# A third buffer of probability rows in fused graph attention, with the softmax two heads ahead and all of its normalising on GpSimd

## The chip, the core and the metric

The kernel runs on one NeuronCore of one Trainium2 chip. The core has five engines that run side by side, each through its own list of instructions in order: TensorE (PE in the profile; its weight loads are shown as PEld), VectorE (DVE), ScalarE (ACT), GpSimd (POOL) and SyncE (SP), which here only starts DMA transfers. An engine waits for another by a semaphore. The metric is the device time of one execution in microseconds (us), and lower is better.

## What is computed

A graph attention layer with 16 heads over 384 nodes, followed by a mixture of eight feed-forward experts. Only the attention is touched by the change. It is, cut from the reference:

```python
q2 = (q @ wiq.T + biq).reshape(N, H, D).transpose(1, 0, 2)   # N = 384, H = 16, D = 64; k2, v2 likewise
scores = jnp.einsum('hnd,hmd->hnm', q2, k2) * scale + mask[None]
attn = jax.nn.softmax(scores, axis=-1)
out = jnp.einsum('hnm,hmd->hnd', attn, v2)
out = out.transpose(1, 0, 2).reshape(N, OUT_F)
return out @ wo.T + bo
```

Everything is float32. The kernel keeps that precision by splitting each matmul operand into a high and a low part (`_hi`, `_lo`) and adding three products.

## The kernel before

The program has four parts that follow each other: six projections in twelve halves (to about 221 us), the attention heads (221.87 to 309.94 us), the output projection with the router (to about 380 us) and the experts. Each engine's order is written out by hand, in one function per engine; there is no scheduler. Semaphores are counted up, and a wait names the count that it needs.

The attention works head by head. A head has three row tiles of 128 nodes by 384 columns (`NT` = 3), and goes through these steps:

- `scores(h)` on TensorE (L1145): for each tile three products of 64 rows into PSUM banks B[0] to B[2]. Tile i of head h waits until `maxima` of head h-1 has read that bank (`score_max`).
- `maxima(h)` on VectorE (L818, L824): mask added, negated scores written to `pr`, row maximum taken. `pr` has two buffers, so head h waits until head h-2 has been transposed (`p_turned`).
- `exps(h)` on ScalarE (L587, L590): the exponential in place in `pr`, row sums into `rsum`.
- normalising: `inverse(h)` on VectorE (L837) takes the reciprocal of the first tile's sums, and GpSimd multiplies that tile (L446); `normalise(h)` on VectorE (L830, L832) takes the reciprocal of the other two and multiplies them itself.
- `turn(h)` on TensorE (L1154, L1161): nine transposes of 128x128 into banks B[3] to B[5], after all three tiles are normalised.
- `at_hi` on ScalarE (L607) and `at_lo` on VectorE (L858) copy the three turned tiles out as high and low part.
- `attend(h)` on TensorE (L1164): nine matmuls with v into bank B[6] or B[7]; then `t_hi` on ScalarE (L599) and `t_lo` on VectorE (L848).

TensorE's loop over h runs `turn(h)`, `attend(h-1)`, `scores(h+2)`. At h = 3, ScalarE and VectorE also split one 1 MB weight chunk for the output projection (L545 and L712, 128x2048); the other chunks of that kind are split after the heads. When `attend(15)` is done (`o_ready` = 16), GpSimd starts `memset(brow_f)` (L451), some constants, and then three additions to `xres` (L471), which VectorE needs for the residual (L881). SyncE's loads of the residual wait for the last scores (L351), those of the output bias for the last `attend` (L356).

Of the kernel before, what the change touches and what calls it, by code (L numbers as in the profile page):

```python
# [30 lines left out]
F32 = mybir.dt.float32  # L31
# [75 lines left out]
def gnn_ffn(nc, x, src, dst, ety, srcb, dstb, ew, wg, bcols, bo, lng, lnb, rw, egc, ebc, wf, b1, b2, be, out):  # L107
    ctx = ExitStack()
    with ctx:
# [19 lines left out]
        with gnn:  # L129
# [7 lines left out]
            with ExitStack() as early:  # L137
                xin = sb(early, "xin", [P, NT, D], F32)
                src_i = sb(early, "src_i", [P, 2, PIECE * P], I32)
                dst_i = sb(early, "dst_i", [P, 2, PIECE * P], I32)  # L140
                keyb = sb(early, "keyb", [P, PIECE * P], F32)
                eqt = sb(early, "eqt", [P, 2, WIN * P], F32)
            k_hi = sb(gnn, "k_hi", [P, KT, N], F32R)
            k_lo = sb(gnn, "k_lo", [P, KT, N], F32R)
            pr = sb(gnn, "pr", [P, 2, NT, N], F32)
# [4 lines left out]
            wterm = sb(gnn, "wterm", [P, 4, EG], F32)  # L150
            bits = sb(gnn, "bits", [P, 2, EG], I32)
            dump = sb(gnn, "dump", [P, EG], F32)
            later = sb(gnn, "later", [P, WIN * P], F32)
# [82 lines left out]
        first_inverse, first_normalised = sem("first_inverse"), sem("first_normalised")  # L236
# [39 lines left out]
        negmax = small[:, 52:58].rearrange("p (b i) -> p b i", b=2)  # L276
        rsum = small[:, 58:64].rearrange("p (b i) -> p b i", b=2)

        rinv = small[:, 64:70].rearrange("p (b i) -> p b i", b=2)
# [125 lines left out]
        def _(pool):  # L405
# [123 lines left out]
        def _(act):  # L529
# [57 lines left out]
            def exps(h):  # L587
                for i in range(NT):
                    act.wait_ge(score_max, NT * h + i + 1)
                    act.activation(pr[:, h % 2, i, :], pr[:, h % 2, i, :], ACT.Exp, scale=-1.0,  # L590
                                   bias=negmax[:, h % 2, i:i + 1], accum_out=rsum[:, h % 2, i:i + 1]).then_inc(exp_done, 1)

            exps(0)
            for h in range(HEADS + 2):
                if h >= 2:

                    o, rows = h - 2, slice(HD * (h % 2), HD * (h % 2) + HD)
                    act.wait_ge(o_ready, o + 1)
                    act.activation(t_hi[rows, o // 2, :], B[6 + h % 2][rows, 0:N], ACT.Identity,  # L599
                                   bias=gbias[rows, 1, o // 2:o // 2 + 1]).then_inc(o_hi_done, 1)  # L600
# [7 lines left out]
                if h + 1 < HEADS:  # L608
                    exps(h + 1)
# [92 lines left out]
        def _(dve):  # L702
# [115 lines left out]
            def maxima(h):  # L818

                if h >= 2:  # L820
                    dve.wait_ge(p_turned, NT * (h - 1))
                for i in range(NT):
                    dve.wait_ge(score_ready, NT * h + i + 1)
                    dve.tensor_tensor_reduce(out=pr[:, h % 2, i, :], in0=B[i][:, 0:N], in1=mask8[:, i, :],  # L824
                                             scale=-SCALE8, scalar=BIG, op0=ALU.add, op1=ALU.min,
                                             accum_out=negmax[:, h % 2, i:i + 1]).then_inc(score_max, 1)

            def normalise(h):
                dve.wait_ge(exp_done, NT * (h + 1))
                link(dve.reciprocal(rinv[:, h % 2, 1:NT], rsum[:, h % 2, 1:NT]))  # L830
                for i in range(1, NT):
                    dve.tensor_scalar(pr[:, h % 2, i, :], pr[:, h % 2, i, :], rinv[:, h % 2, i:i + 1], None,  # L832
                                      ALU.mult).then_inc(normalised, 1)

            def inverse(h):
                dve.wait_ge(exp_done, NT * h + 1)
                dve.reciprocal(rinv[:, h % 2, 0:1], rsum[:, h % 2, 0:1]).then_inc(first_inverse, 1)  # L837
# [566 lines left out]
```

## Time and profile before

| | |
|---|---|
| median of 3 runs | 569.07 us (567.72 to 569.13) |
| the profiled execution | 569.24 us, span 567.5 us |
| busy in the span | PE 513.8 us (91%), DVE 407.6 (72%), ACT 282.3 (50%), POOL 149.1 (26%) |
| mean granted TensorE clock | 0.949 of full |
| chain that ended last | PE 60%, DVE 19%, ACT 8%, POOL 4%, no instruction ("issue") 6% |

The profile covers one execution. Times in a timeline are from the start of the span; the duration of a matmul in it is modelled and overlaps the next, so a run of matmuls is timed from start to start. The chain of waits follows back from the last instruction what released it. The table of stretches gives each engine's busy time within a stretch, and as PEclk the granted clock of TensorE as a part of full speed: 1.00 is 2.4 GHz and 0.50 is 1.2 GHz, its two levels, and what lies between is a stretch with some of both.

### The profile page before, as it was taken

How to read it: one execution, taken by the hardware profiler on the slowest of the kernel's cores; microseconds unless marked ns; L12 is line 12 of the kernel's file. 1: busy time of each engine (PE TensorE's matmuls, PEld its weight loads, DVE VectorE, ACT ScalarE, POOL GpSimd, SP SyncE). 2: the span in 40 equal slices, each digit the busy share in tenths (PEclk: the TensorE clock that was granted, in tenths of full speed). 3: DMA queues.
4: the chain of work that ended last, by engine and by line, in shares of the span. 5: the costliest groups of instructions: out<-in, count | busy, mean ns of one | idle time of the engine just before them, and what ended most of it. 6: DMA issues, size and time to landing. Idle time of an engine off the chain costs nothing.

```text
span 567.5 us, 6818 instructions
## 1 busy us (share of the span) xinstructions
PE 513.8 (91%) x2579; PEld 445.8 (79%) x2579; DVE 407.6 (72%) x675; ACT 282.3 (50%) x407; POOL 149.1 (26%) x129
## 2 busy tenths in 40 slices
PE   3899999999999998989998979449999999999994
PEld 3899889999999998878787868437776776776773
DVE  6658877744334435789997867775987987987995
ACT  2435223423323443677776104335787687687540
POOL 5100333542334330122223922222012022000362
PEclk9899999999999999689999989658999999999988
DMA  8278663333443343010006521495859889879452
GB/s 308 107 267 361 230 234 136 118 130 126 150 149 105 118 151 114 1 74 2 0 1 209 179 62 69 137 343 205 319 220 397 318 328 390 330 288 374 149 185 112
DMA packets 20929, 106.32 MB, mean 187 GB/s; under 512 B 4720, under 2 KB 5104, under 8 KB 11168
## 3 DMA queue, kind: packets, MB, share of 16 engines
q1 hardware_dynamic: 15328, 91.53, 42.6%
q0 software_dynamic: 3696, 7.96, 4.3%
q10 hardware_dynamic: 1872, 6.39, 3.1%
q8 instruction: 21, 0.34, 0.2%
q14 instruction: 12, 0.10, 0.1%
HBM read 98.96 MB, written 6.91 MB: 187 GB/s over the span
## 4 chain that ended last, share of the span: by engine, by line
PE 60%; DVE 19%; ACT 8%; issue 6%; POOL 4%; DMA 1%; ACTq 0%; DVEq 0%; POOLq 0%
PE ps L1098 53%; DVE lo L712 10%; PE ps L1161 3%; ACT xg L629 3%; POOL xres L471 2%; ACT hi L545 2%; PE ps L1201 2%; DVE hh L1022 1%; ACT xg_hi L633 1%; DMA xg<-z_rows,slot_tok 1%; DVE small L717 1%; ACT sg L638 1%; DMA xin<-in_x 1%; DVE x2c L1011 1%; DVE ht_lo L977 1%
## 5 line engine op out<-in xcount | busy, mean ns | idle before, releaser
L712 DVE TENSOR_TENSOR lo<-raw,hi 128x2048 fp32r<-128x2048 f32 x70 | 159.2, 2289 | 60.6 <-ACT hi L545 60.5
L545 ACT ACTIVATE hi<-raw 128x2048 fp32r<-128x2048 f32 x70 | 131.7, 1913 | 76.0 <-PE ps L1098 65.1
L438 POOL DMA_INDIRECT mask_rows<-colf,bits x48 | 56.2, 1171 | 134.7 <-DMA mask_rows<-colf,bits 83.0
L1098 PE MATMUL ps<-xt_hi,hi 128*128 128x384 f32 x192 | 65.2, 339 | 2.3 <-DVE xt_lo L728 2.3
L1098 PE MATMUL ps<-xt_hi,lo 128*128 128x384 f32 x192 | 65.2, 340 | 0.0
L1098 PE MATMUL ps<-xt_lo,hi 128*128 128x384 f32 x192 | 65.2, 340 | 0.0
L1098 PE MATMUL ps<-hi,xg_hi 128*128 128x512 f32 x128 | 53.1, 415 | 1.5 <-DVE xg_lo L972 1.5
L1098 PE MATMUL ps<-lo,xg_hi 128*128 128x512 f32 x128 | 51.3, 401 | 0.0
L1098 PE MATMUL ps<-hi,xg_lo 128*128 128x512 f32 x128 | 51.2, 400 | 0.0
L1098 PE MATMUL ps<-t_hi,lo 128*128 128x384 f32 x128 | 43.0, 336 | 0.0
L1098 PE MATMUL ps<-t_lo,hi 128*128 128x384 f32 x128 | 43.0, 336 | 0.0
L1098 PE MATMUL ps<-t_hi,hi 128*128 128x384 f32 x128 | 43.0, 336 | 0.0
L446 POOL TENSOR_SCALAR pr<-pr,small 128x384 f32<-128x384 f32 x16 | 19.9, 1246 | 76.2 <-DVE small L837 76.2
L1098 PE MATMUL ps<-hi,t_hi 128*128 128x512 f32 x96 | 39.0, 406 | 0.0
L1098 PEld LDWEIGHTS ps<-xt_hi,hi 128*128 128x128 f32 x192 | 36.7, 191 | 2.6 <-issue 2.6
L1098 PE MATMUL ps<-hi,t_lo 128*128 128x512 f32 x96 | 38.6, 402 | 0.0
L1098 PE MATMUL ps<-lo,t_hi 128*128 128x512 f32 x96 | 38.6, 402 | 0.0
L1098 PEld LDWEIGHTS ps<-xt_hi,lo 128*128 128x128 f32 x192 | 36.6, 191 | 0.0
L1098 PEld LDWEIGHTS ps<-xt_lo,hi 128*128 128x128 f32 x192 | 36.5, 190 | 0.0
L1098 PEld LDWEIGHTS ps<-hi,xg_hi 128*128 128x128 f32 x128 | 24.7, 193 | 10.8 <-issue 5.6
L607 ACT ACTIVATE at_hi<-ps 128x384 fp32r<-128x384 f32 x48 | 20.7, 492 | 24.0 <-PE ps L1161 23.1
L1161 PE MATMUL ps<-ident,pr 128*128 128x128 f32 x144 | 21.8, 303 | 9.9 <-issue 3.9
(207 smaller groups left out, 1065.8 us busy)
## 6 DMA issues: line engine op xcount, KB each, us to landing
raw<-in_wf SPq DMA_DIRECT2D x42, 1024.0 KB, 7.2
raw<-in_wg SPq DMA_DIRECT2D x28, 1024.0 KB, 5.4
xfb<-in_wf SPq DMA_DIRECT2D x6, 1024.0 KB, 7.3
src_i<-in_srcb ACTq DMA_DIRECT2D x4, 768.0 KB, 4.9
dst_i<-in_dstb ACTq DMA_DIRECT2D x4, 768.0 KB, 9.9
y_rows<-y SPq DMA_DIRECT2D x6, 512.0 KB, 3.0
xin<-in_x SPq DMA_DIRECT2D x3, 512.0 KB, 4.6
xres<-in_x SPq DMA_DIRECT2D x3, 512.0 KB, 4.8
```

The costliest lines, as they stand in the source:

```text
L438: pool.indirect_dma_start(out=mbuf[:, :], out_offset=bass.IndirectOffsetOnAxis(ap=bits[:, 1, g:g + 1], axis=0), in_=colf[:, 5, g:g + 1], i ...
L446: pool.tensor_scalar(pr[:, h % 2, 0, :], pr[:, h % 2, 0, :], rinv[:, h % 2, 0:1], None, ALU.mult).then_inc(first_normalised, 1)
L471: pool.tensor_tensor(xres[:, t, :], xres[:, t, :], bob, ALU.add).then_inc(resid_ready, 1)
L545: act.activation(hi[SLOT[c]][:, :], raws[RAW[c]], ACT.Copy).then_inc(hi_done, 1)
L607: act.activation(at_hi[:, h % 2, j, :], B[3 + j][:, 0:N], ACT.Copy).then_inc(at_hi_done, 1)
L629: ins = act.activation(xg[:, par, k * P:(k + 1) * P], B[5 + a][:, (k % 4) * P:(k % 4 + 1) * P], ACT.Identity, scale=egb[:, 0, e, k:k + 1], ...
L633: act.activation(xg_hi[:, par, 4 * a:4 * a + 4, :].rearrange("p k n -> p (k n)"), xg[:, par, a * CW:(a + 1) * CW], ACT.Copy).then_inc(xg_h ...
L638: act.activation(sg[:, :], x2c[:, :], ACT.Silu).then_inc(silu_done, 1)
L712: dve.tensor_tensor(lo[SLOT[c]][:, :], raws[RAW[c]], f32(hi[SLOT[c]][:, :]), ALU.subtract).then_inc(lo_done, 1)
L1098: ins = pe.matmul(o, a[s], b[m], start=first and n == 0, stop=last and n == 2)
L1161: ins = pe.transpose(B[3 + j][:, i * P:(i + 1) * P], pr[:, h % 2, i, j * P:(j + 1) * P], ident[:, :])
L1201: ins = pe.matmul(B[0][:, t * NE:(t + 1) * NE], xft[:, k, :], rws[:, k, :], start=k == 0, stop=k == KT - 1)
```

## The change

`pr` and the small columns beside it (`negmax`, `rsum`, `rinv`) get a third buffer, indexed by h % 3. To make room, three tensors that are used only before the attention (`wterm`, `dump`, `later`) move to memory that k_hi and its neighbours reuse. TensorE issues `scores(h+3)` instead of `scores(h+2)`, with `scores(2)` ahead of the loop. ScalarE does `exps(h+2)` instead of `exps(h+1)`, and `t_hi` of a head at the end of a turn of its loop instead of at the start of the next. VectorE does `maxima(h+2)` and only the reciprocals, in two instructions; the multiplications L832 are gone from it. GpSimd does three multiplications for each head instead of one. The diff, without the moved tensors:

```diff
-            pr = sb(gnn, "pr", [P, 2, NT, N], F32)
+            pr = sb(gnn, "pr", [P, 3, NT, N], F32)
...
             for h in range(HEADS):
-                pool.wait_ge(first_inverse, h + 1)
-                pool.tensor_scalar(pr[:, h % 2, 0, :], pr[:, h % 2, 0, :], rinv[:, h % 2, 0:1], None,
-                                   ALU.mult).then_inc(first_normalised, 1)
+                for i in range(NT):
+                    if i < 2:
+                        pool.wait_ge(inverse_ready, 2 * h + i + 1)
+                    pool.tensor_scalar(pr[:, h % 3, i, :], pr[:, h % 3, i, :], rinv[:, h % 3, i:i + 1], None,
+                                       ALU.mult).then_inc(normalised, 1)
...
             exps(0)
-            for h in range(HEADS + 2):
-                if h >= 2:
-
-                    o, rows = h - 2, slice(HD * (h % 2), HD * (h % 2) + HD)
-                    act.wait_ge(o_ready, o + 1)
-                    act.activation(t_hi[rows, o // 2, :], B[6 + h % 2][rows, 0:N], ACT.Identity,
-                                   bias=gbias[rows, 1, o // 2:o // 2 + 1]).then_inc(o_hi_done, 1)
+            exps(1)
+            for h in range(HEADS + 1):
                 if h == 3:
                     split_hi(OUT_LAST - 1)
...
-                if h + 1 < HEADS:
-                    exps(h + 1)
+                if h + 2 < HEADS:
+                    exps(h + 2)
+                if h >= 1:
+
+                    o, rows = h - 1, slice(HD * ((h - 1) % 2), HD * ((h - 1) % 2) + HD)
+                    act.wait_ge(o_ready, o + 1)
...
-                if h >= 2:
-                    dve.wait_ge(p_turned, NT * (h - 1))
+                if h >= 3:
+                    dve.wait_ge(p_turned, NT * (h - 2))
...
+            def inverse(h, tiles, done):
+                dve.wait_ge(exp_done, NT * h + done)
+                dve.reciprocal(rinv[:, h % 3, tiles], rsum[:, h % 3, tiles]).then_inc(inverse_ready, 1)
+
+            FIRST_TILE, OTHERS = (slice(0, 1), 1), (slice(1, NT), NT)
             maxima(0)
-            inverse(0)
-            normalise(0)
+            inverse(0, *FIRST_TILE)
+            maxima(1)
+            inverse(0, *OTHERS)
+            inverse(1, *FIRST_TILE)
+            inverse(1, *OTHERS)
             for h in range(HEADS + 2):
-                if h + 1 < HEADS:
-                    maxima(h + 1)
+                if h + 2 < HEADS:
+                    maxima(h + 2)
...
                     for j in range(NT):
-                        if j == NT - 1 and h + 1 < HEADS:
-                            inverse(h + 1)
+                        if j == NT - 1 and h + 2 < HEADS:
+                            inverse(h + 2, *FIRST_TILE)
...
-                if h + 1 < HEADS:
-                    normalise(h + 1)
+                if h + 2 < HEADS:
+                    inverse(h + 2, *OTHERS)
...
             def turn(h):
-                pe.wait_ge(first_normalised, h + 1)
-                pe.wait_ge(normalised, (NT - 1) * (h + 1))
+                pe.wait_ge(normalised, NT * (h + 1))
...
             scores(0)
             scores(1)
+            scores(2)
             for h in range(HEADS + 1):
                 if h < HEADS:
                     turn(h)
                 if h >= 1:
                     attend(h - 1)
-                if h + 2 < HEADS:
-                    scores(h + 2)
+                if h + 3 < HEADS:
+                    scores(h + 3)
```

VectorE within one head in the middle, before. The names are the tiles: `t_lo` is the output of an earlier head, `at_lo` the low part of the turned tiles of head h, `small` the columns of sums and reciprocals; the L824 rows at the end begin `maxima` of the next head.

```order
L848 SCALAR_TENSOR_TENSOR t_lo<-ps,gbias,t_hi 64x384 [waits o_hi_done]
L858 TENSOR_TENSOR at_lo<-ps,at_hi 128x384 [waits at_hi_done] x2
L837 RECIPROCAL small<-small 128x1 [waits exp_done]
L858 TENSOR_TENSOR at_lo<-ps,at_hi 128x384 [waits at_hi_done]
L830 RECIPROCAL small<-small 128x2 [waits exp_done]
L832 TENSOR_SCALAR pr<-pr,small 128x384 [waits dve_chain]
L832 TENSOR_SCALAR pr<-pr,small 128x384
L824 ISA pr,small<-ps,mask 128x384 [waits score_ready,p_turned]
```

The same place in the changed kernel (L827 is the old L824, L833 both reciprocals):

```order
L848 SCALAR_TENSOR_TENSOR t_lo<-ps,gbias,t_hi 64x384 [waits o_hi_done]
L858 TENSOR_TENSOR at_lo<-ps,at_hi 128x384 [waits at_hi_done] x2
L833 RECIPROCAL small<-small 128x1 [waits exp_done]
L858 TENSOR_TENSOR at_lo<-ps,at_hi 128x384 [waits at_hi_done]
L833 RECIPROCAL small<-small 128x2 [waits exp_done]
L827 ISA pr,small<-ps,mask 128x384 [waits score_ready,p_turned]
```

The two multiplications L832 are gone, and the reciprocals now belong to head h+2 instead of h+1.

TensorE at the start of the attention, before: the last tile of `scores(1)`, `turn(0)`, and the first tile of `scores(2)`. `k_hi` and `xt_hi` are keys and queries, `ident,pr` is a transpose.

```order
L1098 MATMUL ps<-k_hi,xt_hi 128x384 [waits score_max]
L1098 MATMUL ps<-k_lo,xt_hi 128x384
L1098 MATMUL ps<-k_hi,xt_lo 128x384
L1161 MATMUL ps<-ident,pr 128x128 [waits normalised,first_normalised]
L1161 MATMUL ps<-ident,pr 128x128 x8
```

The same piece in the changed kernel, where the rows ahead of `turn(0)` are the last two tiles of `scores(2)`:

```order
L1098 MATMUL ps<-k_hi,xt_hi 128x384 [waits score_max]
L1098 MATMUL ps<-k_lo,xt_hi 128x384
L1098 MATMUL ps<-k_hi,xt_lo 128x384
L1098 MATMUL ps<-k_hi,xt_hi 128x384 [waits score_max]
L1098 MATMUL ps<-k_lo,xt_hi 128x384
L1098 MATMUL ps<-k_hi,xt_lo 128x384
L1160 MATMUL ps<-ident,pr 128x128 [waits normalised]
```

The nine matmuls of `scores(2)` stand ahead of `turn(0)` instead of behind it, and every `scores` after that is one head earlier. GpSimd's list has 48 multiplications (L448) in place of 16 (L446), and the rest of it is unchanged, as is SyncE's.

## Rows read from the trace of the kernel before

**Rows 1.** Table of stretches, cut at starts of `turn`: stretch, length, busy time (count), PEclk, DMA

```profile
221.87:238.53 16.66, 15.23 (x63) 13.58 (x63) 11.52 (x39) 9.44 (x26) 3.77 (x3) 0.69 0.00 0
238.53:243.24 4.71, 4.57 (x29) 4.03 (x28) 3.79 (x13) 4.07 (x11) 1.24 (x1) 1.00 0.01 3
243.24:250.32 7.08, 4.53 (x28) 3.98 (x28) 6.95 (x16) 4.94 (x11) 1.25 (x1) 0.98 0.21 74
250.32:256.30 5.98, 5.98 (x28) 5.47 (x28) 4.83 (x17) 3.84 (x10) 1.24 (x1) 0.73 0.22 89
256.30:295.70 39.40, 36.26 (x217) 31.90 (x217) 36.39 (x111) 28.94 (x80) 9.95 (x8) 1.00 0.00 1
295.70:300.78 5.08, 4.52 (x27) 3.98 (x28) 4.77 (x15) 3.63 (x10) 1.25 (x1) 1.00 0.00 0
300.78:305.61 4.83, 2.77 (x19) 2.48 (x19) 4.45 (x15) 3.61 (x10) 1.24 (x1) 1.00 0.91 314
305.61:309.94 4.33, 4.33 (x28) 4.33 (x29) 2.65 (x5) 1.83 (x4) 0.00 (x0) 1.00 0.76 254
```

**Rows 2.** Chain of waits, one head: start, length, what

```profile
265.98 1.18 PE ps L1161 x9
267.15 3.35 PE ps L1098 x18
270.50 0.56 issue
```

**Rows 3.** Timeline, two heads: start, length, engine, line, operation [idle before]

```profile
260.31 0.75 DVE L832 TENSOR_SCALAR pr<-pr,small 128x384 f32<-128x384 f32 x2
...
264.10 1.24 POOL L446 TENSOR_SCALAR pr<-pr,small 128x384 f32<-128x384 f32 x1 [3.69 <-DVE small L837]
...
264.98 0.90 DVE L832 TENSOR_SCALAR pr<-pr,small 128x384 f32<-128x384 f32 x2
```

**Rows 4.** Groups by line, 224 to 308 us: busy us, mean ns | idle before

```profile
L590 ACT ACTIVATE pr<-pr,small 128x384 f32<-128x384 f32 x48 | 29.0, 612 | 1.2 <-DVE small L824 1.1
...
L824 DVE CUSTOM_DVE_ANT_0 pr<-ps,mask 128x384 f32<-128x384 f32 x46 | 23.1, 548 | 0.2 <-PE ps L1098 0.2
...
L607 ACT ACTIVATE at_hi<-ps 128x384 fp32r<-128x384 f32 x48 | 20.7, 492 | 24.0 <-PE ps L1161 23.1
```

**Rows 5.** GpSimd's multiplication, line L446 alone: ns min/median/max, first and last start

```profile
L446 POOL TENSOR_SCALAR pr<-pr,small x16: 1242/1244/1263, 224.5 to 303.7; 128x384 f32<-128x384 f32 x16
```

**Rows 6.** GpSimd's longest instructions after the heads, line L471 alone: ns min/median/max

```profile
L471 POOL TENSOR_TENSOR xres<-xres,xfb x3: 3392/3874/4452, 315.5 to 322.7; 128x1024 f32<-128x1024 f32 x3
```

**Rows 7.** Timeline at the start of the attention

```profile
224.26 0.16 DVE L837 RECIPROCAL small<-small 128x1 f32<-128x1 f32 x1
...
224.54 1.26 POOL L446 TENSOR_SCALAR pr<-pr,small 128x384 f32<-128x384 f32 x1 [15.66 <-DVE small L837]
...
225.36 0.17 DVE L830 RECIPROCAL small<-small 128x2 f32<-128x2 f32 x1 [0.94 <-ACT pr L590]
...
226.48 2.15 PE L1161 MATMUL ps<-ident,pr 128*128 128x128 f32 x9 [1.20 <-DVE pr L832]
```

**Rows 8.** Table of stretches where the granted clock was low

```profile
226.60:236.20 9.60, 9.37 (x34) 8.56 (x35) 6.98 (x23) 6.22 (x17) 1.86 (x2) 0.50 0.00 0
...
247.70:250.20 2.50, 0.06 (x1) 0.00 (x0) 2.46 (x8) 0.51 (x2) 1.25 (x1) 0.98 0.57 197
250.20:253.20 3.00, 2.88 (x12) 2.91 (x13) 2.89 (x10) 1.68 (x4) 0.00 (x0) 0.50 0.46 186
```

**Rows 9.** Timeline of the weight chunk that is split at h = 3

```profile
242.78 1.92 ACT L545 ACTIVATE hi<-raw 128x2048 fp32r<-128x2048 f32 x1
...
245.25 2.29 DVE L712 TENSOR_TENSOR lo<-raw,hi 128x2048 fp32r<-128x2048 f32 x1
```

**Rows 10.** Chain of waits after the last head

```profile
309.99 1.80 POOL brow_f L451
...
315.50 11.62 POOL xres L471 x3
```

More of the change, by code:

```diff
@@ L142, in gnn_ffn @@
                 eqt = sb(early, "eqt", [P, 2, WIN * P], F32)
+                wterm = sb(early, "wterm", [P, 4, EG], F32)
+                dump = sb(early, "dump", [P, EG], F32)
+                later = sb(early, "later", [P, WIN * P], F32)
             k_hi = sb(gnn, "k_hi", [P, KT, N], F32R)
             k_lo = sb(gnn, "k_lo", [P, KT, N], F32R)
-            pr = sb(gnn, "pr", [P, 2, NT, N], F32)
+            pr = sb(gnn, "pr", [P, 3, NT, N], F32)
             at_hi = sb(gnn, "at_hi", [P, 2, NT, N], F32R)
@@ L275, in gnn_ffn @@
         halfneg = small[:, 48:49]
-        negmax = small[:, 52:58].rearrange("p (b i) -> p b i", b=2)
-        rsum = small[:, 58:64].rearrange("p (b i) -> p b i", b=2)
-        rinv = small[:, 64:70].rearrange("p (b i) -> p b i", b=2)
+        negmax = small[:, 52:61].rearrange("p (b i) -> p b i", b=3)
+        rsum = small[:, 61:70].rearrange("p (b i) -> p b i", b=3)
+        rinv = small[:, 0:9].rearrange("p (b i) -> p b i", b=3)
         SCALE8 = 1.0 / 8.0
@@ L818, in maxima @@
             def maxima(h):
[L820 to L821 removed]
+                if h >= 3:
+                    dve.wait_ge(p_turned, NT * (h - 2))
                 for i in range(NT):
                     dve.wait_ge(score_ready, NT * h + i + 1)
[L824 removed]
+                    dve.tensor_tensor_reduce(out=pr[:, h % 3, i, :], in0=B[i][:, 0:N], in1=mask8[:, i, :],
                                              scale=-SCALE8, scalar=BIG, op0=ALU.add, op1=ALU.min,
[L826 to L837, printed above, removed]
[L839 to L841 removed]
+                                             accum_out=negmax[:, h % 3, i:i + 1]).then_inc(score_max, 1)
+            def inverse(h, tiles, done):
+                dve.wait_ge(exp_done, NT * h + done)
+                dve.reciprocal(rinv[:, h % 3, tiles], rsum[:, h % 3, tiles]).then_inc(inverse_ready, 1)
+            FIRST_TILE, OTHERS = (slice(0, 1), 1), (slice(1, NT), NT)
+            maxima(0)
+            inverse(0, *FIRST_TILE)
[3 more added lines that the diff above has]
+            inverse(1, *OTHERS)
             for h in range(HEADS + 2):
[L843 to L844 removed]
+                if h + 2 < HEADS:
+                    maxima(h + 2)
                 if h >= 2:
@@ L1160, in turn @@
                     for i in range(NT):
-                        ins = pe.transpose(B[3 + j][:, i * P:(i + 1) * P], pr[:, h % 2, i, j * P:(j + 1) * P], ident[:, :])
+                        ins = pe.transpose(B[3 + j][:, i * P:(i + 1) * P], pr[:, h % 3, i, j * P:(j + 1) * P], ident[:, :])
                     ins.then_inc(p_turned, 1)
```

11 lines of the change are left out of this document (5 added, 6 removed).

## The prediction, made before the changed kernel was run

> **What bounds the kernel now.** I read the table of stretches first, cut at the starts of `turn`, because only the attention changes. The last matmul of the attention starts it off at 221.87 us and ends it at 309.94 us, 88.07 us in all [rows 1]. In the middle, the eight heads from `turn(5)` to `turn(13)` take 39.40 us, 4.925 us each. VectorE is busy for 36.39 us of that and TensorE for 36.26 us [rows 1], so two engines look full. The chain of waits tells them apart: nine transposes take 1.18 us and the eighteen matmuls behind them 3.35 us, 4.53 us in all, and then TensorE stands for up to 0.56 us [rows 2]. That is a loop over three engines. After `turn(h)` ScalarE copies the tiles (3 x 0.49 us) and then takes the exponentials of head h+1 (3 x 0.61 us) [rows 4], VectorE then multiplies two tiles (0.75 us, or 0.90 us in the next head) [rows 3], and only then can `turn(h+1)` go. TensorE's own 4.53 us is the floor underneath.
>
> Three more places lose time. The first two heads up to `turn(2)` take 16.66 us, at a mean clock of 0.69 [rows 1]: the granted clock was 0.50, that is 1.2 GHz, for 9.60 us [rows 8], after TensorE had stood for 1.20 us ahead of `turn(0)` [rows 7]. Head 3 takes 7.08 us [rows 1], since the weight chunk holds ScalarE for 1.92 us and then VectorE for 2.29 us [rows 9] in the same loop; TensorE stands idle for nearly all of 2.50 us, and the clock is then 0.50 for 3.00 us more [rows 8], so head 4 takes 5.98 us. At the end, the heads after `turn(13)` take 5.08 and 4.83 us up to `turn(15)`, though the second has only 2.77 us of TensorE work [rows 1].
>
> What is behind the attention hangs on its end: GpSimd starts at 309.99 us and runs into the 11.62 us of `xres` additions [rows 10]. SyncE's list is the same, its residual loads wait for the last scores, which come a head earlier, and all else for the last `attend`. A gain in the attention passes on in full.
>
> **The middle.** Removed from VectorE are two multiplications per head, 0.75 to 0.90 us [rows 3]; 36.39 / 8 = 4.55 us of work becomes 3.65 to 3.80. ScalarE does the same work, 28.94 / 8 = 3.62 us per head [rows 1]. GpSimd goes from one to three multiplications, 3 x 1.244 = 3.73 us [rows 5]; a handover from the reciprocal took 224.54 - 224.42 = 0.12 us [rows 7], so at most 3.97. All are under 4.53.
>
> Does the loop still hold? Count from the start of `turn(h)`. The copies are done at about 1.8 us (0.55 us until the first, then 3 x 0.42 from start to start, an estimate from the length of three overlapping instructions), the exponentials of head h+2 at 1.8 + 1.9 = 3.7, the reciprocals at 3.9, and GpSimd's last two tiles at 3.9 + 0.1 + 2 x 1.244 = 6.5, call it 6.6. They are needed at `turn(h+2)`, at 9.06. `maxima(h+2)` can start when the reciprocals of head h+1 are done, 3.9 - 4.53 = -0.6, and ends near 0.6 behind the last score tile; ScalarE asks for it at 1.8, and `scores(h+3)` at 2.8. What queues behind the new waits of VectorE, the third `at_lo` and the next `maxima`, has 1 us to spare or more. So nothing is late, and TensorE's 4.53 us becomes the period: from `turn(5)` to `turn(13)` 39.40 - 36.24 = **3.2 us gained**. For the period I keep 4.40 to 4.60 as bounds: 4.40 if some of the 3.35 us still holds small waits, 4.60 if 0.07 is lost between `scores` and `turn`, where the trace shows no boundary without a wait.
>
> **Heads 2 to 4.** `turn(2)` to `turn(3)` took 4.71 us, 0.2 over the period. At h = 3 ScalarE now has 0.2 us in hand, so its copies come 1.7 us late and end at 3.0 us after `turn(3)`. VectorE does the chunk from 1.75 to 4.05 us, then two `at_lo` to 5.1 and the third to 5.65. `turn(4)` may begin at 4.53 and needs those banks freed one by one: it ends about 0.4 us late. The exponentials of head 5 are not wanted for another head. With this wait shortened to 0.4 us the idle 2.5 us and the low clock behind it go as well. Here one unknown remains: this subtraction reads two SBUF tensors while GpSimd is busy far more than before. The nearest row is GpSimd's L471, which took 3392 to 4452 ns [rows 6] with VectorE busy beside part of it, so neighbours may cost something. GpSimd's tiles for head 4 end about 2.05 us after `turn(3)` and its next begin at 5, so the two would meet for 0.3 us. I take 0.3, with 0 and one whole multiplication, 1.25 us, as bounds. Total stall 0.7 us. `turn(2)` to `turn(5)` goes from 17.77 [rows 1] to 3 x 4.53 + 0.7 = 14.3: **3.5 us gained**.
>
> On this place the Trainium skill (SBUF — State Buffer, "Who interferes with whom") says that a VectorE instruction with two SBUF inputs contends with a GpSimd instruction that reads SBUF, and that the later one stands until the other is through. By that rule the stall would be 0.4 plus whatever is left of one multiplication; and the pair L832, which took 0.90 us when it began at 264.98 beside a GpSimd multiplication that ran until 265.34, and 0.75 us in the head before, agrees in kind [rows 3]. [...]
>
> **The tail.** `turn(15)` now waits for GpSimd, not for TensorE: `maxima(15)` and `exps(15)` lie in turn 13 of the loops, so by the count above it starts 6.6 us after `turn(13)`, where TensorE alone would need 2 x (1.18 + 1.76) = 5.9. It took 5.08 + 4.83 = 9.91 us [rows 1]. **3.3 us gained.** The last 4.33 us stay.
>
> **The start** goes the other way. `scores(2)` and `maxima(1)` move ahead of the second reciprocal of head 0, which could be made at 225.36 [rows 7] and now follows three L824 at some 0.48 us from start to start, at 226.1. GpSimd's first tile ends at 225.8 [rows 7], the others at 226.2 + 2 x 1.25 = 228.7, so `turn(0)` starts at 228.75 instead of 226.48 [rows 7]. Head 1's three tiles end at 228.7 + 3.75 = 232.45, head 2's at 236.2. TensorE stands from 226.5 to 228.75, and in both places of the trace where it stood the clock came back at half [rows 7, 8]. At half, `turn(0)` takes 2.15 [rows 7], `scores(3)` 3.0, and `turn(1)` runs from 233.9. If the clock returns at 236.4 as in the trace (the low 9.60 us [rows 8] plus its edges), `turn(2)` starts at 239.4; with a first transpose block still at full speed 239.1. If it returns after about 3 us, as in the second place [rows 8], 237.5; with no drop at all 237.0, by GpSimd's pace; with ten low us that start later, 240.5. I take 239.0, near the longer case since that is the same place of the program: **0.5 us lost**, although one more `scores` is done by then (which the tail gives back).
>
> **Sum.** 3.2 (middle) + 3.5 (heads 2 to 4) + 3.3 (tail) - 0.5 (start) = 9.5 us. The attention ends at 300.4, and the profiled 569.24 us become **559.7 us**. The profiled execution is 0.17 us above the median of the three runs, 569.07, so no correction is made. Its own range: start 237.0 to 240.5, stall 0.4 to 1.65, period 4.40 to 4.60 over eleven heads, and 1 us of spread behind the attention as the runs have (567.72 to 569.13); not all at one end, 557.0 to 563.
>
> **Rivals.** (a) The low clock comes back. TensorE was busy for 9.37 of 9.60 us and stayed at 0.50 [rows 8], so work alone did not raise it at once; the many heads at 1.00 [rows 1] speak against. A second such stretch costs half of 10.2 us: 559.7 + 5.1 = 564.8. (b) Another loop holds the heads near 4.9 us, for instance VectorE's waits in the middle of its list: 11 x 0.4 = 4.4 us of the gain is gone, 564.1. The slack of 1 us counted above speaks against. (c) GpSimd is slowed by its neighbour as L471 may have been, 1.244 x 4452 / 3392 = 1.63 us per tile: 48 x 1.63 from 224.54 is 302.8, with handovers 304.5, near the old `turn(15)` at 305.6. That is 568. All sixteen multiplications ran in 1242 to 1263 ns [rows 5] beside VectorE's work, which speaks against. (d) Slower: each GpSimd multiplication first has to wait out a VectorE instruction, 0.55 us [rows 4]: 1.79 us a tile, 48 x 1.79 + 224.54 = 310.5 against 305.61, 4.9 us later, 574.1. This mechanism decides the sign from (305.61 - 224.54) / 48 = 1.69 us a tile; the measured 1.244 is far below.
>
> **How the numbers follow.** Forecast 72%, (a) 9%, (b) 9%, (c) 5%, (d) 5%. Faster by over 0.3% (1.7 us, about what a measurement of this kernel can tell from no change) are the forecast, (a) and (b): 0.90. Same is (c): 0.05. Slower is (d): 0.05. The range must leave out no more than 20%. It leaves out (c), (d), the longer half of (a), and the edge of the forecast: 557.0 to 564.5.
>
> **What would show it.** In the changed kernel: `turn` every 4.5 to 4.6 us from `turn(5)` on with no idle time of TensorE ahead of it; L448 at 1.24 to 1.3 us, three in a row; no gap of 2.5 us at h = 3 and a clock of 1.00 around 250 us; `turn(0)` near 228.7 with idle time released by POOL; GpSimd as what ends the wait of `turn(15)`; the last `attend` near 300.4. A period over 4.7 or an L448 over 1.45 us would prove the middle wrong, a clock of 0.50 after 240 us the start.

## The result, and the profile after

| | before | after |
|---|---|---|
| median, us | 569.09 | 559.28 |
| lowest to highest, runs | 567.72 to 569.13, 4 | 558.90 to 561.25, 4 |
| profiled execution, us | 569.24 | 561.25 |
| its span, us | 567.5 | 559.5 |
| attention, first scores to last matmul | 88.07 | 79.51 |

The ratio of the times is 0.983 [0.981, 0.985], so the changed kernel is 9.8 us faster; 559.7 was predicted. The profiled execution is the longest of the four. Two other profiles of the same kernel (first experiment) have an attention that is 1.6 us shorter, all of it in the first two heads. Their first scores come 1.3 to 1.5 us later (at 222.96 and 222.77 us, not 221.51), so their spans are only 0.8 and 0.9 us shorter. The part of the span behind the attention is 257.5 us before and 258.4 in this profile (257.7 and 257.9 in the other two): the gain does pass on, to within 0.9 us.

Here is the table of stretches of the changed kernel, cut at the starts of `turn`, with the columns of [rows 1]. After the stretch and its length come the busy time (and count) of PE, PEld, DVE, ACT and POOL, and then PEclk, DMA and GB/s. The cuts are at the first scores, `turn(0)`, `turn(1)`, `turn(2)`, `turn(3)`, `turn(4)`, `turn(5)`, `turn(13)` and `turn(15)`:

```profile
221.51:228.22 6.71, 4.92 (x28) 4.52 (x28) 4.72 (x21) 4.14 (x13) 3.80 (x4) 1.00 0.00 0
228.22:233.45 5.23, 5.23 (x19) 4.46 (x19) 2.66 (x10) 3.26 (x9) 5.23 (x5) 0.51 0.00 0
233.45:240.34 6.89, 6.89 (x29) 6.19 (x29) 3.68 (x12) 3.84 (x10) 5.34 (x5) 0.63 0.01 2
240.34:244.90 4.56, 4.56 (x29) 4.06 (x29) 3.65 (x13) 3.99 (x11) 2.27 (x3) 1.00 0.00 0
244.90:249.50 4.60, 4.39 (x27) 3.85 (x27) 4.29 (x8) 4.58 (x11) 1.78 (x2) 1.00 0.01 2
249.50:254.28 4.78, 4.78 (x28) 3.97 (x29) 4.78 (x19) 4.21 (x11) 4.29 (x4) 1.00 0.61 219
254.28:290.12 35.84, 35.84 (x218) 31.81 (x218) 30.66 (x99) 28.96 (x80) 30.68 (x26) 1.00 0.01 1
290.12:296.65 6.53, 5.33 (x36) 4.87 (x36) 5.46 (x15) 5.33 (x14) 5.53 (x5) 1.00 0.81 283
296.65:301.02 4.37, 4.37 (x28) 4.37 (x29) 2.42 (x5) 1.83 (x4) 0.00 (x0) 1.00 0.47 177
```

A cut may stand 0.14 us beside the true start: the timeline has `turn(2)` at 240.28, `turn(3)` at 244.76, `turn(5)` at 254.21 and `turn(13)` at 290.05. I use those below. In the seventh row TensorE is busy for all of 35.84 us, where [rows 1] had 36.26 of 39.40; VectorE has fallen from 36.39 to 30.66 us and GpSimd has risen from 9.95 to 30.68 us. No wait of another engine is left. The chain of waits (start, length, what) in the middle and at the end says the same, and answers to [rows 2, 10]:

```profile
258.76 1.13 PE ps L1160 x9
259.90 3.36 PE ps L1098 x18
263.25 1.13 PE ps L1160 x9
...
292.91 3.70 POOL pr L448 x3
296.61 0.04 issue
296.65 1.20 PE ps L1160 x9
297.86 3.16 PE ps L1098 x18
301.02 0.05 issue
301.07 1.80 POOL brow_f L453
```

Nine transposes and eighteen matmuls now stand edge to edge, 1.13 + 3.36 = 4.49 us a head. In this piece only `turn(15)` hangs on GpSimd's three multiplications, which take 3.70 us with nothing between them. The line of that multiplication alone (ns min/median/max, first and last start) answers to [rows 5]:

```profile
L448 POOL TENSOR_SCALAR pr<-pr,small x48: 1239/1246/1264, 224.2 to 295.4; 128x384 f32<-128x384 f32 x48
```

Forty-eight of them, and the longest took 1264 ns: none was held up by VectorE. The timeline of the start and of the weight chunk (start, length, engine, line, operation, idle time before it and what ended it) answers to [rows 7, 9]:

```profile
228.22 2.11 PE L1160 MATMUL ps<-ident,pr 128*128 128x128 f32 x9 [1.79 <-POOL pr L448]
...
243.00 3.69 POOL L448 TENSOR_SCALAR pr<-pr,small 128x384 f32<-128x384 f32 x3 [2.29 <-DVE small L833]
...
246.47 2.29 DVE L715 TENSOR_TENSOR lo<-raw,hi 128x2048 fp32r<-128x2048 f32 x1 [0.25 <-ACT hi L547]
...
249.50 1.45 PE L1160 MATMUL ps<-ident,pr 128*128 128x128 f32 x9 [0.21 <-DVE at_lo L858]
```

The first line is the new wait at `turn(0)`: 1.79 us for GpSimd, and the nine transposes behind it take 2.11 us instead of the 1.20 that this view gives them at full clock, since the clock is at half. The last line is all that is left of the 2.50 us that TensorE stood at h = 3 [rows 8]: 0.21 us for the third `at_lo`.

### The profile page after: what moved, and what is told of

Same layout as the page of the kernel before. It is cut to its first block, busy times and chain, and to the rows that moved or that the text cites. A ratio compares the mean times of both kernels' runs of the same rounds, so it can differ in the third digit from the quotient of the medians.

```text
span 559.5 us, 6816 instructions
## 1 busy us (share of the span) xinstructions
PE 513.0 (92%) x2579; PEld 445.1 (80%) x2579; DVE 394.6 (71%) x643; ACT 282.3 (50%) x407; POOL 187.7 (34%) x161
## 4 chain that ended last, share of the span: by engine, by line
PE 60%; DVE 19%; ACT 9%; issue 6%; POOL 5%; DMA 1%; ACTq 0%; DVEq 0%; POOLq 0%
PE ps L1098 53%; DVE lo L715 10%; ACT xg L632 3%; PE ps L1160 3%; ACT hi L547 2%; POOL xres L473 2%; PE ps L1201 2%; POOL pr L448 1%; DVE hh L1022 1%; ACT xg_hi L636 1%; DMA xg<-z_rows,slot_tok 1%; PE ps L1194 1%; DVE small L720 1%; ACT sg L641 1%; DVE x2c L1011 1%
## 5 line engine op out<-in xcount | busy, mean ns | idle before, releaser
L448 POOL TENSOR_SCALAR pr<-pr,small 128x384 f32<-128x384 f32 x48 | 58.9, 1247 | 29.3 <-DVE small L833 29.3
L492 POOL CAST selx<-sels 48x128 fp32r<-48x128 f32 x8 | 3.4, 436 | 93.7 <-PE ps L1098 89.7
L592 ACT ACTIVATE pr<-pr,small 128x384 f32<-128x384 f32 x48 | 29.0, 612 | 1.2 <-DVE small L827 1.1
```

Of the source, the lines that this page charges most:

```text
L448: pool.tensor_scalar(pr[:, h % 3, i, :], pr[:, h % 3, i, :], rinv[:, h % 3, i:i + 1], None, ALU.mult).then_inc(normalised, 1)
L592: act.activation(pr[:, h % 3, i, :], pr[:, h % 3, i, :], ACT.Exp, scale=-1.0, bias=negmax[:, h % 3, i:i + 1], accum_out=rsum[:, h % 3, i:i ...
```

## Experiments

The question of all of them: the change has two halves, a deeper pipeline and a move of two multiplications from VectorE to GpSimd. Which one brings the gain, and what does each cost? The theory on record is that the loop over three engines set the old period, so depth would do it. The first rival is that VectorE, at 36.39 of 39.40 us [rows 1], was the bound, and the move does it. "Attention" is from here on from the first scores to the start of `brow_f` on GpSimd, 88.12 us before.

### The changed kernel again

No edit. Two more groups of runs, on other occasions (the second beside the last two versions below), to see which part of the first profile repeats.

> The changed kernel once more, unaltered, as the pair for the runs beside it and for a second profile. Expected 558.9 to 561.3 us. The first profile is of the longest of four executions: from the end of the last attend (301.02 us) to the end of the span it took 258.5 us, against 257.6 us in the kernel before. If that 0.9 us is chance, as I think, this profile has 257 to 258 us there and the attention still ends near 301; if it belongs to the change, it has 258.5 again.

Measured: 560.19 us (559.05 to 560.68), ratio 0.982 [0.980, 0.984]. The attention took 78.00 us, where the first profile had 79.56. The first three stretches:

```profile
222.96:229.68 6.72, 4.91 (x28) 4.53 (x28) 4.73 (x21) 4.13 (x13) 3.80 (x4) 1.00 0.00 0
229.68:233.63 3.95, 3.95 (x19) 3.35 (x19) 2.10 (x8) 3.03 (x9) 3.95 (x4) 0.70 0.00 0
233.63:240.18 6.55, 6.55 (x28) 6.06 (x28) 4.08 (x14) 3.83 (x10) 6.27 (x6) 0.66 0.01 3
```

`turn(0)` comes 6.72 us after the first scores, as before; what differs is how the low clock falls on what follows (0.70 and 0.66, against 0.51 and 0.63). In the first profile the granted clock was 0.50 from 228.4 to 238.5 us, 10.1 us from the first transposes on. Here the transposes of `turn(0)` run at full speed, and it is 0.50 from about 231.3 to 238.0 us, 6.7 us. `turn(2)` is 17.22 us after the start, not 18.77. Behind the attention this profile has 257.7 us, so most of the 0.9 us more of the first one does not repeat and is no cost of the change. The other group repeats all this.

> The changed kernel once more, on the same chip as the runs beside it: 559 to 560.5 us.

Measured: 559.45 us (559.10 to 560.35), ratio 0.983 [0.981, 0.985]; attention 77.98 us, `turn(2)` 17.20 us after the start. So 78.0 us is the usual attention of this kernel, and the first profile's 1.6 us more is a variation of when the clock is low. I don't know what decides that.

### Depth alone

Three buffers and the new order stay. GpSimd multiplies only the first tile, as before the change, and VectorE the other two; `turn` waits for both.

```diff
-                for i in range(NT):
+                for i in range(1 if h in VECTOR else NT):      # VECTOR = range(HEADS)
...
+            def others(h):
+                inverse(h, *OTHERS)
+                if h in VECTOR:
+                    dve.wait_ge(inverse_ready, 2 * h + 2)
+                    for i in range(1, NT):
+                        dve.tensor_scalar(pr[:, h % 3, i, :], pr[:, h % 3, i, :], rinv[:, h % 3, i:i + 1], None,
+                                          ALU.mult).then_inc(vector_normalised, 1)
...
-                    inverse(h + 2, *OTHERS)
+                    others(h + 2)
...
```

> One part alone: three buffers, scores three ahead and softmax two ahead stay, but VectorE multiplies the second and third tile of every head again (from its own list, after their reciprocals) and GpSimd only the first. My theory: the gain comes from the depth, which takes the loop ScalarE, VectorE, TensorE apart; the move to GpSimd is only there to get VectorE's work per head (3.8 us in the changed kernel, 4.55 us with the two multiplications) under TensorE's 4.48. So the period is 4.5 to 4.75 us and the time 555 to 563 us, with a turn(0) near 226.5 us instead of 228.2 as an extra. Rival: the gain comes from the unloading of VectorE; then the period stays at 4.9 us and the time at 563 us or more.

Measured: 559.35 us (559.20 to 560.27), ratio 0.982 [0.980, 0.984]; attention 78.09 us. The stretches are the first two heads, then head 3 and head 4, then the eight of the middle, then the two of the tail:

```profile
221.81:235.08 13.27, 12.34 (x73) 10.93 (x73) 11.87 (x43) 10.84 (x32) 4.03 (x4) 1.00 0.00 0
...
239.57:245.91 6.34, 4.53 (x28) 3.98 (x28) 6.21 (x14) 5.17 (x11) 0.99 (x1) 1.00 0.00 1
245.91:252.18 6.27, 6.27 (x27) 5.28 (x28) 6.20 (x20) 3.87 (x10) 2.49 (x2) 0.73 0.46 167
252.18:288.01 35.83, 35.83 (x217) 31.80 (x216) 35.33 (x110) 29.11 (x80) 8.81 (x8) 1.00 0.01 1
288.01:295.32 7.31, 5.80 (x37) 4.91 (x37) 7.17 (x21) 5.02 (x13) 2.46 (x2) 1.00 0.85 284
```

The middle is 35.83 us with the move undone: the same 4.48 us a head for TensorE. So it was the loop that held the heads at 4.93 us, and not the length of VectorE's list. But VectorE is now the next bound, and it is already the slower of the two. Its pair of multiplications in the turn of the loop ahead of `turn(5)` and the one eight heads later, and then TensorE at `turn(14)` (start, length, engine, line, operation, idle time before it and what ended it):

```profile
251.37 0.99 DVE L841 TENSOR_SCALAR pr<-pr,small 128x384 f32<-128x384 f32 x2
...
288.45 0.99 DVE L841 TENSOR_SCALAR pr<-pr,small 128x384 f32<-128x384 f32 x2
...
292.26 1.44 PE L1172 MATMUL ps<-ident,pr 128*128 128x128 f32 x9 [1.48 <-DVE at_lo L867]
```

VectorE needs 37.08 / 8 = 4.64 us a head, so it falls 0.16 us a head behind TensorE and lives on the lead that the depth gives it. The debt comes due in the tail, where `turn(14)` stands for 1.48 us until the third `at_lo`. With many more heads VectorE would set the pace, by these rows at 4.64 us (an estimate); with the move it is busy for 30.66 / 8 = 3.83 us a head. All versions with three buffers also have `t_hi` at its new place in ScalarE's loop and the scores three heads ahead; what each of these is worth alone was not tested, and "depth" here means all of them together.

The total is equal to that of the changed kernel because differences cancel. At the start depth alone is better by 3.9 us (`turn(2)` 13.27 us after the first scores, not 17.2, at a clock of 1.00). At the weight chunk it is worse by about 3.2 us (heads 3 and 4 take 12.61 us, 9.45 with the move), since VectorE has no slack from which to pay the 2.29 us of the subtraction, and in the tail by 0.7 (7.31 against 6.60).

### The move alone

Two buffers, one head ahead, the old order, and GpSimd multiplies all three tiles.

```diff
-                pool.wait_ge(first_inverse, h + 1)
-                pool.tensor_scalar(pr[:, h % 2, 0, :], pr[:, h % 2, 0, :], rinv[:, h % 2, 0:1], None,
-                                   ALU.mult).then_inc(first_normalised, 1)
+                for i in range(NT):
+                    if i < 2:
+                        pool.wait_ge(inverse_ready, 2 * h + i + 1)
+                    pool.tensor_scalar(pr[:, h % 2, i, :], pr[:, h % 2, i, :], rinv[:, h % 2, i:i + 1], None,
+                                       ALU.mult).then_inc(normalised, 1)
...
-                for i in range(1, NT):
-                    dve.tensor_scalar(pr[:, h % 2, i, :], pr[:, h % 2, i, :], rinv[:, h % 2, i:i + 1], None,
-                                      ALU.mult).then_inc(normalised, 1)
```

> The other part alone: the kernel before with two buffers and the softmax one head ahead, but GpSimd multiplies all three tiles. My theory: two multiplications of 1.25 us then stand in the loop in place of 0.8 us on VectorE, so turn comes every 6.5 to 6.7 us and the time is 590 to 600 us, more if TensorE's clock falls in the waits. Rival (unloading VectorE is what helped): 569 us or less.

Measured: 597.94 us for its one run, some 29 us slower than before; attention 115.27 us, some 6.5 us a head. Its chain of waits walks once round the loop in a head:

```profile
263.97 0.56 PE ps L1159 x3
...
264.56 1.26 ACT at_hi L609 x3
...
265.83 0.72 ACT pr L592 x2
...
266.58 0.17 DVE small L836
...
266.83 3.70 POOL pr L448 x3
```

This is the loop of the prediction's first part, with GpSimd's three multiplications in place of VectorE's two. In the changed kernel the same 3.70 us sit in the same place and cost nothing in the middle, because one more head of TensorE's work lies between the exponentials and the `turn` that needs them. Moving work to a slower engine without the depth loses three times what the change gains.

### How near GpSimd is to being the bound

Rival (c) said that GpSimd's pace could decide. Two more multiplications per head, which alter nothing that is read later, bring it over the 4.49 us of TensorE.

```diff
+                for cut in (slice(0, 6), slice(0, 2)):
+                    link(pool.tensor_scalar(colf[:, cut, :], colf[:, cut, :], rinv[:, h % 3, 0:1], None, ALU.mult))
```

> The changed kernel, with two more multiplications by GpSimd behind the three of each head, on 288 and 96 columns of a tensor that is no longer needed (colf), each awaited. GpSimd's work per head goes from 3.75 us to about 5.2 us (estimate: 0.95 and 0.4 us for the two, 0.1 for each wait). My theory: GpSimd has 0.7 us to spare below TensorE's 4.48 us, and from there on sets the period alone; turn(15) starts at 224.2 + 15 x 5.25 + 3.7 = 306.7 us instead of 296.6, and the time is near that of the kernel before, 567 to 571 us. Rival (another engine still holds the period, GpSimd's work is hidden up to 5 us): under 563 us.

Measured: 576.01 us (575.85 to 576.17), ratio 1.011 [1.009, 1.013]: slower than before the change, and past what I expected. One head in the chain of waits, then the line alone, then the timeline at the weight chunk:

```profile
264.22 3.69 POOL pr L448 x3
267.90 0.98 POOL colf L451
...
268.98 0.53 POOL colf L451
```

```profile
L448 POOL TENSOR_SCALAR pr<-pr,small x48: 1237/1244/3042, 224.5 to 309.6; 128x384 f32<-128x384 f32 x48
```

```profile
246.30 5.48 POOL L448 TENSOR_SCALAR pr<-pr,small 128x384 f32<-128x384 f32 x3
...
247.16 2.29 DVE L717 TENSOR_TENSOR lo<-raw,hi 128x2048 fp32r<-128x2048 f32 x1 [0.25 <-ACT hi L549]
```

GpSimd's head is 3.69 + 0.98 + 0.53 us and 0.17 us between them, 5.37 us, and `turn` follows at 5.37 us from its start to the next. The mechanism is right, and the size was not: I had given a head 5.25 us. `turn(15)` came at 310.94 us and not at 306.7, mostly by 0.12 us a head and the one long multiplication below, and TensorE then took 6.07 us to the end at a clock of 0.72, where the changed kernel took 4.37. By these rows, per head GpSimd has 4.49 - 3.70 = 0.8 us in hand, and beyond that it sets the pace; only the one point beyond was tested.

One multiplication took 3042 ns. The three ran from 246.30 to 251.78, so by the lengths the second began near 247.55, with VectorE's subtraction of two SBUF tensors under way until 249.45. Standing until then and taking 1.2 us would end it at 250.65; 247.55 + 3.04 is 250.59. That is the rule of the Trainium skill (SBUF — State Buffer, "Who interferes with whom") that the prediction weighed, in numbers: 1.8 us lost by the later one. The other direction doesn't show. In the changed kernel that subtraction began at 246.47 with GpSimd busy until 243.00 + 3.69 = 246.69, and here at 247.16 with GpSimd's first multiplication running until about 247.54, and it took 2.29 us both times, the mean of its line. It may be that the overlap was too short to see.

### VectorE for head 0 alone

The start is where GpSimd's three tiles in a row are on the path. So the edit of "Depth alone", with one head:

```diff
-        VECTOR = range(HEADS)
+        VECTOR = (0,)
```

> The changed kernel, with the second and third tile of head 0 alone multiplied by VectorE. Theory: TensorE's 1.8 us of standing ahead of turn(0), while GpSimd works through three tiles, is what brings the granted clock down to 1.2 GHz for some 10 us; with turn(0) at 226.7 us, as in e_depth, the clock stays at 1.00, turn(1) waits for GpSimd until 230.6, turn(2) starts near 235.1 instead of 240.3, and the time is 553.5 to 555 us. Rival: e_depth kept its clock since VectorE paced all heads; then the clock falls here too, turn(2) starts at 239 or later, and the time is over 558 us.

Measured: 555.98 us (555.12 to 557.37), ratio to before 0.977 [0.975, 0.979], so 3 to 4 us under the changed kernel. The expected 553.5 to 555 was missed upward, though the heads did what the theory said: the part behind the attention took 258.5 us in this profile. Up to `turn(0)`, `turn(1)` and `turn(2)`:

```profile
222.93:227.88 4.95, 4.90 (x28) 4.47 (x28) 3.97 (x17) 3.84 (x12) 1.27 (x1) 1.00 0.00 0
227.88:231.75 3.87, 2.96 (x19) 2.47 (x19) 3.28 (x14) 3.33 (x11) 3.76 (x4) 1.00 0.00 0
231.75:236.24 4.49, 4.49 (x27) 3.98 (x27) 3.81 (x14) 3.50 (x10) 4.49 (x4) 1.00 0.00 0
```

`turn(0)` starts 4.95 us after the first scores with no wait to speak of, the clock stays at 1.00, and `turn(2)` comes at 13.31 us, not 17.2. The attention is 74.11 us.

### Transposes that fill the wait

That gain has two causes mixed: the wait itself, and the low clock after it. This separates them. GpSimd keeps all tiles, and sixteen identity transposes into a free bank keep TensorE at work until `turn(0)`.

```diff
+            keep_warm(B[6], 16)        # after scores(2), ahead of turn(0)
```

> The changed kernel, with 16 transposes of the identity into an unused bank (B[6]) between scores(2) and turn(0), which is 1.7 us of work at full speed in the 1.8 us in which TensorE stood. Theory: the clock then stays at 1.00; turn(0) does not start earlier, turn(1) is released by GpSimd at about 232.0 and turn(2) starts near 236.5 instead of 240.3: 555 to 556.5 us. Rival (the low clock comes from what TensorE does before turn(0), not from the standing): low clock as before, 559 to 561 us.

Measured: 556.70 us (555.39 to 557.96), ratio 0.978 [0.976, 0.979]; attention 75.65 us.

```profile
221.73:228.44 6.71, 6.71 (x43) 6.21 (x43) 4.73 (x21) 4.13 (x13) 3.79 (x4) 1.00 0.00 0
228.44:232.10 3.66, 2.98 (x19) 2.49 (x18) 1.79 (x7) 3.03 (x9) 3.66 (x4) 1.00 0.00 0
```

`turn(0)` stands where it stood, 6.71 us after the start, and the clock stays at 1.00. So the low clock costs 78.00 - 75.65 = 2.35 us of the changed kernel, and the wait for GpSimd in head 0 a further 75.65 - 74.11 = 1.54 us. These are differences between single profiles. The whole times agree on the first (the expected 555 to 556.5 was missed by 0.2 us); the second, 556.70 against 555.98, is too small for them.

The same in the kernel before, with eleven transposes:

> The kernel before, with 11 such transposes between scores(1) and turn(0), in place of 1.2 us of standing. It tells how much of the 9.8 us the clock alone is worth without the change. Theory: the clock stays at 1.00 there, and the first two heads are then paced by the loop at 4.9 us each: turn(2) at 236.4 instead of 238.5, 2 us less than the kernel before, 566.5 to 568 us. Rival: the low clock is the main loss of the kernel before, 564 us or less.

Measured: 569.49 us (566.43 to 570.32), ratio 1.000 [0.998, 1.001]. A miss. The first row below runs from `turn(0)` to `turn(2)`, which comes 13.96 us after the first scores at 222.59, not 16.66 [rows 1], with the clock at 1.00: 2.7 us earlier. Then it gives it all back:

```profile
227.20:236.55 9.35, 7.46 (x47) 6.46 (x46) 7.75 (x27) 6.53 (x19) 2.51 (x2) 1.00 0.00 0
...
248.45:255.61 7.16, 7.16 (x27) 6.47 (x28) 5.15 (x17) 3.84 (x10) 1.25 (x1) 0.59 0.20 82
...
304.95:310.93 5.98, 5.98 (x28) 5.95 (x29) 2.75 (x5) 2.02 (x5) 0.00 (x0) 0.71 0.54 184
```

Head 4 takes 7.16 us at 0.59, where it was 5.98 at 0.73 [rows 1], and the last stretch 5.98 at 0.71, where it was 4.33 at 1.00. The idle 2.5 us of head 3 and the wait ahead of `turn(15)` are still there, and the low clock now stands behind both. In this kernel the repair of this one wait did not pay; in the changed kernel, where only the 1.2 us ahead of `turn(15)` are left besides, it does.

### VectorE for the first and the last head

The tail, too, waits for three GpSimd tiles in a row.

```diff
-        VECTOR = (0,)
+        VECTOR = (0, HEADS - 1)
```

> As e_start, and also the second and third tile of head 15 by VectorE. Theory: turn(15) then waits for nothing and starts 5.9 us after turn(13) instead of 6.5; 0.6 us less than e_start, 553 to 554.5 us. Rival: turn(15) was held by something besides GpSimd, and it stays at 6.5.

Measured: 556.03 us (555.04 to 557.59), ratio 0.977 [0.975, 0.979]. From `turn(13)` to `turn(15)` it is

```profile
284.83:290.71 5.88, 5.42 (x37) 4.99 (x37) 5.11 (x15) 5.18 (x14) 3.17 (x3) 1.00 0.75 265
```

5.88 us against 6.60. That is not yet TensorE alone, as the expectation had it: `turn(15)` now stands for the third `at_lo`:

```profile
290.71 1.39 PE L1172 MATMUL ps<-ident,pr 128*128 128x128 f32 x9 [0.47 <-DVE at_lo L867]
```

The attention is 73.56 us, 0.55 less than with head 0 alone, but the median is not lower, and the expected 553 to 554.5 us was missed: half a microsecond can't be told in the whole time. A second group of runs of the same version:

> e_ends once more, unaltered, on the same chip: 3 to 4 us less than the changed kernel beside it. Its attention took 73.56 us, against 79.56 and 78.00 us in two profiles of the changed kernel.

Measured: 556.12 us (554.74 to 557.68), ratio 0.976 [0.974, 0.979], with the changed kernel at 559.45 beside it: 3.3 us below it.

### One tile of each head for VectorE

GpSimd takes the first and the third tile of every head, VectorE the second. Against the changed kernel, with `others` as above:

```diff
-                for i in range(NT):
-                    if i < 2:
-                        pool.wait_ge(inverse_ready, 2 * h + i + 1)
+                for i in (0, 2):
+                    pool.wait_ge(inverse_ready, 2 * h + 1 + i // 2)
...
-                    for i in range(1, NT):
+                    for i in (1,):
```

> The changed kernel, with the work of normalising split evenly in every head: GpSimd multiplies the first and third tile, VectorE the second. Theory: VectorE's work per head is then 3.8 + 0.4 = 4.2 us and GpSimd's 2.5 us, both under TensorE's 4.48; turn(0) comes 5.3 us after the first scores (6.7 in the changed kernel, 4.95 in e_ends), so TensorE stands for 0.5 us only and the clock stays at 1.00; turn(15) comes 5.9 us after turn(13). The attention takes 74 us against 78.0 to 79.6 in the changed kernel, and the time is 554.5 to 556.5 us. Rival: VectorE's multiplication meets GpSimd's at the memory port (0.99 us for two in e_depth beside GpSimd, 0.75 alone) in each head, and the period rises to 4.6 us or more: 557 us or more.

Measured: 555.62 us (554.37 to 557.31), ratio 0.976 [0.974, 0.979]; attention 73.41 us, the shortest (74 was expected). The period is 4.48 us once more. `turn(0)` came 5.84 us after the first scores, not 5.3, after 0.92 us of standing, and the clock stayed at 1.00. The tail, `turn(13)` to `turn(15)`, and GpSimd's line alone:

```profile
285.06:290.81 5.75, 5.63 (x37) 4.90 (x37) 5.29 (x16) 4.85 (x14) 3.93 (x4) 1.00 0.81 276
```

```profile
L448 POOL TENSOR_SCALAR pr<-pr,small x32: 1239/1244/1484, 224.6 to 289.4; 128x384 f32<-128x384 f32 x32
```

All three versions with some work back on VectorE lie within 0.5 us of one another, and their intervals overlap; none is shown to be the best. All beat both kernels.

## Why the prediction was right, point by point

| place | before | predicted | three profiles of after |
|---|---|---|---|
| first scores to `turn(2)` | 16.66 | 17.1 | 18.77, 17.22, 17.20 |
| `turn(2)` to `turn(5)` | 17.77 | 14.3 | 13.93 in the first and the second |
| `turn(5)` to `turn(13)` | 39.40 | 36.24 | 35.84 in the first, 35.83 in the second |
| `turn(13)` to `turn(15)` | 9.91 | 6.6 | 6.60 in the first, 6.61 in the second |
| last stretch | 4.33 | 4.33 | 4.37 in the first |

**The middle.** Right in cause, and the term was 0.4 us too small: the period is 4.48 us, not 4.53, so the chain before still held some 0.05 us a head of small waits, within the bounds of 4.40 to 4.60. That the loop and not VectorE was the bound is shown by "Depth alone" (4.48 us with VectorE's work undiminished) and from the other side by "The move alone". The prediction counted that VectorE must be unloaded too; for sixteen heads the middle did not need it, since the lead of two heads covered the 0.16 us a head by which VectorE fell behind.

**Heads 2 to 4.** Predicted stall 0.7 us, found 13.93 - 3 x 4.48 = 0.5. The chunk came where the working put it. The 0.4 us for the third `at_lo` is 0.21 us in the timeline. The 0.3 us for a meeting of VectorE's subtraction with GpSimd's next multiplication did not occur. The two engines overlapped only at the other end, for 0.2 us while GpSimd finished the tiles of head 4, and neither was longer for it. The pair L832, which the prediction took as agreeing in kind with the rule for two SBUF inputs, reads one SBUF tensor in each instruction: it is a case of its own. That both the move and the depth are needed here, the prediction did not say; "Depth alone" shows it, 12.6 us for heads 3 and 4 against 9.45.

**The tail.** 6.6 predicted and 6.60 found, with GpSimd as what `turn(15)` waits for. The 5.9 us for TensorE alone was too much: without the wait of 1.21 us the profile has 5.39 (`turn(13)` at 290.05, `turn(14)` at 292.65, `turn(15)` at 296.65). That nothing rested on it is luck; the 5.88 us with VectorE on the last head have 0.47 us of waiting in them.

**The start.** `turn(0)` came 6.71 us after the first scores in all three profiles, predicted 6.88. The loss up to `turn(2)` is 0.55 us in two of them, predicted 0.5, and 2.1 us in the first. The prediction had that case as its bound, ten low microseconds that start later, and set it at 240.5, or 18.6 us after the first scores; the 18.77 lie just past it. In the two others the number is right by a low stretch of another shape than the one counted: it began later and lasted 6.7 us, not 9.6. In the first profile the granted clock was 0.50 from `turn(0)` on, until about 238.5 us:

```profile
229.00:237.00 8.00, 8.00 (x30) 7.23 (x29) 4.72 (x15) 5.59 (x15) 6.48 (x6) 0.50 0.00 0
```

The reason that the prediction gave, that the clock came back at half "in both places of the trace where it stood", overlooks a third place. Ahead of `turn(15)` TensorE stood for 2.06 us in the kernel before, and the 4.33 us behind it ran at 1.00 [rows 1]; in the changed kernel it stood there for 1.21 us, again with 1.00 behind it. So standing is not all that decides. That filling the wait at `turn(0)` keeps the clock up is shown; why a wait at `turn(15)` did no harm is open.

I also missed that the start is not a small item. I compared it with the kernel before, which has its own low clock there; compared with the best that the same order allows, it costs 3.9 us, nearly half of the whole gain. My count moved `turn(0)` by 2.3 us, and the experiments show 1.5 us for the wait and 2.35 for the clock.

**Behind the attention.** Passed on, to within the 1 us allowed: what follows took 258.4, 257.7 and 257.9 us against 257.5. No room was allowed for the part ahead of the attention, which moved as much: the first scores came at 221.51, 222.96 and 222.77 us in three profiles of one kernel.

**The rivals.** (a) No clock of 0.50 between 240 us and the end of the attention in the changed kernel; but where VectorE had no slack at the chunk it did come back, 0.73 in head 4 of "Depth alone". (b) No other loop: TensorE is busy for 35.84 of 35.84 us. (c) and (d): all 48 multiplications took 1239 to 1264 ns, so neither happened. "How near GpSimd is" showed that (d)'s direction is real: with 5.37 us of GpSimd work a head the kernel is slower than before, 576.0 us.

The sum was off in parts that cancel: the middle and heads 2 to 4 gave 0.8 us more than predicted, and the rest behind the attention took back 0.2 to 0.9. In the two later profiles the attention is 78.0 us, 10.1 under 88.12, against a predicted gain of 9.5. The whole gained 9.8 us in the medians but 8.0 in the two profiled executions, so that the median of 559.28 us falls within 0.5 us of the forecast is in part luck.

## What to carry to other kernels

When two engines look nearly full, follow the chain of waits through one period before believing either: a chain that walks through several engines in each head, as that of "The move alone" does, is a loop, and depth removes it whichever engine does the work. In the kernel before, the chain showed only TensorE and "issue" [rows 2], so there the loop had to be counted and then tested. Work may then go to a slower engine as long as its sum per period stays under the bound (here 3.7 of 4.5 us), but at the first and last round of the loop, where nothing lies over it, the fast engine should keep it. Once the loop is gone, compare the cycle of each engine, and not only its busy share, with the bound: one that is slower by 0.16 us a head stays hidden as long as the lead lasts. And count the clock behind a wait with the wait.

## What the runs showed of the hardware

- TensorE stood for 1.20 us ahead of `turn(0)` before [rows 7] and 1.8 us after, and each time the granted clock went to half (1.2 GHz) behind it, for 9.6 us before and for 10.1, 6.7 and about 6.8 us in three profiles after, although TensorE was busy for nearly all of that. With no more than 0.93 us of idle time in 13.27 us at the same place ("Depth alone"), or with the wait filled, it stayed at 1.00. Ahead of `turn(15)` it stood for 2.06 us before and 1.21 us after, and the clock stayed at 1.00: the length of one wait does not tell.
- A cure of one such wait in the kernel before moved the low clock to two later waits, which had been followed by a shorter one or by none, and the time did not change (ratio 1.000).
- A GpSimd multiplication that began during VectorE's 2.29 us subtraction of two SBUF tensors took 3042 ns, not 1244. With one tile of each head on VectorE, one GpSimd multiplication took 1484 ns. In the changed kernel, where VectorE has none of them, no tile of 48 was over 1264. The other way round, VectorE's pair of multiplications, 0.75 us alone, took 0.99 us in "Depth alone" when it began 0.5 us into a GpSimd multiplication of 1.25 us (250.90 us): 0.24 us more, though 0.8 us of that multiplication were still to come.
